# Gate and up weight units: transposed on VectorE instead of TensorE, in a quartered layout and a new schedule

## The reference

```
x = x + linear0(cond0(x))      cond0: rows of a sample times W[cond_id] (64 x 64)
                               linear0: x @ (W + sum of 8 LoRA products).T + bias, 1024 -> 1024
x = x + down(silu(gate(c)) * up(c)),   c = adapter(x): rank-16 product B, A of the sample's adapter id
gate, up: 2752 x 1024, down: 1024 x 2752, as NF4 codes (int32, 0 to 15):
    W[o, i] = NF4[codes[o, i]] * scales[o, i // 64]
```

## Time and profile before

| | |
|---|---|
| Median of three runs | 1036.76 us (1036.56 to 1037.09) |
| Profiled execution, its own time | 1037.4 us |
| Its span | 1035.5 us |
| First and last L948 start (phase A) | 41.1 and 349.4 us |
| Matmuls at L982 | 520 (65 units of 8) |
| VectorE L735, mean of one | 1233 ns, x260 |
| VectorE L737, mean of one | 1230 ns, x195 |
| ScalarE L566, mean of one | 1051 ns, x455 |
| DMA, mean over the span | 122 GB/s |

### The profile page before, as it was taken

How to read it: one execution, slowest core, us unless ns; L and a number is a source line. 1 busy time by engine, 2 the same in 40 slices (tenths; PEclk the granted TensorE clock), 3 DMA queues, 4 the chain that set the end, 5 groups by cost and what they waited for, 6 DMA issues and landing times.

```text
span 1035.5 us, 14607 instructions
## 1 busy us (share of the span) xinstructions
PE 1005.8 (97%) x5368; PEld 858.6 (83%) x5368; DVE 841.6 (81%) x834; ACT 793.5 (77%) x946; POOL 223.2 (22%) x269
## 2 busy tenths in 40 slices
PE   4999999999999899999999999999999999999998
PEld 3898898998898777788888888888888888888886
DVE  3999999989999889978887788887887879784344
ACT  4788887888888779888888888888887878884120
POOL 4014434324322301120111111111122112112000
PEclk9999999999999999999999999999999999999999
DMA  9844455446432436755654645655464545565666
GB/s 249 245 119 127 113 138 124 104 139 149 104 104 62 82 61 122 132 100 115 118 106 82 114 95 98 121 102 103 82 122 87 103 96 109 95 102 143 162 223 225
DMA packets 65397, 126.27 MB, mean 122 GB/s; under 512 B 6544, under 2 KB 38816, under 8 KB 65328
## 3 DMA queue, kind: packets, MB, share of 16 engines
q0 software_dynamic: 15200, 51.41, 31.9%
q1 hardware_dynamic: 48800, 72.88, 23.1%
q10 hardware_dynamic: 1328, 1.05, 0.3%
HBM read 66.61 MB, written 67.11 MB: 129 GB/s over the span
## 4 chain that ended last, share of the span: by engine, by line
PE 84%; DVE 9%; ACT 3%; issue 2%; DMA 1%; ACTq 0%; DVEq 0%
PE ps_z L1074 21%; PE ps_y L1074 21%; PE ps_z L948 13%; PE ps_gu L1053 11%; PE ps_t L982 5%; DVE val L735 4%; PE ps_t L990 3%; PE ps_gu L990 3%; DVE val L737 3%; PE ps_y L935 2%; PE ps_gu L965 2%; ACT ring L566 1%; PE ps_t L957 1%; DMA la<-in_L_ffn_lora_A 1%; DVE val L754 1%
## 5 line engine op out<-in xcount | busy, mean ns | idle before, releaser
L566 ACT ACTIVATE ring<-codes 128x1024 f32<-128x1024 int32 x455 | 452.6, 1051 | 17.9 <-DVE val L735 17.8
L735 DVE TENSOR_TENSOR val<-val,ring 128x1024 f32<-128x1024 f32 x260 | 320.6, 1233 | 36.3 <-ACT ring L566 20.4
L737 DVE SCALAR_TENSOR_TENSOR val<-ring,val 128x1024 f32<-128x1024 f32 x195 | 239.9, 1230 | 39.4 <-ACT ring L566 31.5
L539 POOL DMA_DIRECT2D out<-staged x80 | 68.8, 860 | 315.3 <-ACT staged L685 307.9
L866 DVE TENSOR_TENSOR inter<-ps_gu,inter 128x512 f32<-128x512 f32 x88 | 60.5, 687 | 74.5 <-ACT inter L671 74.5
L671 ACT ACTIVATE inter<-ps_gu 128x512 f32<-128x512 f32 x88 | 52.4, 595 | 71.8 <-PE ps_gu L1053 69.3
L948 PE MATMUL ps_z<-we_hi,y_hi 128*128 128x512 f32 x256 | 104.8, 409 | 0.5 <-DVE y_lo L785 0.5
L948 PE MATMUL ps_z<-we_hi,y_lo 128*128 128x512 f32 x256 | 100.4, 392 | 0.0
L948 PE MATMUL ps_z<-we_lo,y_hi 128*128 128x512 f32 x256 | 99.9, 390 | 0.0
L677 ACT ACTIVATE in_hi<-inter 128x512 fp32r<-128x512 f32 x88 | 55.4, 630 | 48.1 <-DVE inter L866 48.1
L481 POOL TENSOR_TENSOR st_hi<-ga_f,one 128x128 fp32r<-128x128 f32 x42 | 40.7, 968 | 218.1 <-ACT ga_f L606 218.1
(11 more groups left out here) (130 smaller groups left out, 1856.6 us busy)
## 6 DMA issues: line engine op xcount, KB each, us to landing
out<-staged POOLq DMA_DIRECT2D x80, 512.0 KB, 5.4
codes<-in_L_ffn_gate_codes SPq DMA_DIRECT2D x21, 512.0 KB, 4.9
codes<-in_L_ffn_up_codes SPq DMA_DIRECT2D x21, 512.0 KB, 4.2
codes<-in_L_ffn_down_codes SPq DMA_DIRECT2D x21, 512.0 KB, 4.0
xs<-in_x SPq DMA_DIRECT2D x16, 512.0 KB, 4.3
out<-in_L_ffn_bias SPq DMA_DIRECT2D x4, 2048.0 KB, 13.4
out<-xs POOLq DMA_DIRECT2D x16, 512.0 KB, 5.5
ring<-out SPq DMA_DIRECT2D x16, 512.0 KB, 4.6
```

The costliest lines, as they stand in the source:

```text
L539: pool.dma_start(out_rows[t * P:(t + 1) * P, :], staged[:, place, :], accum_op=ALU.add).then_inc(acc_out[place], 16)
L566: act.activation(ring[:, (k - 1) % RING, :], codes[:, n % 2, :], ACT.Identity, bias=offset, scale=slope).then_inc(lines, 1)
L735: ins = dve.tensor_tensor(v, v, line, pick)
L737: ins = dve.scalar_tensor_tensor(out=v, in0=line, scalar=add, in1=v, op0=ALU.add, op1=pick)
```

## The change

- A gate or up unit is loaded in quarters: partition block a (32 partitions) holds columns 256a to 256a + 255 of all 128 rows, rows i * 32 + p side by side. So each 32 x 32 block, transposed by VectorE's block transpose within its partitions, gives the columns on the partitions, in the layout that `adapter_ga` reads. The transpose is a ninth step of these units, for which `turn_unit` and `evac_wt` are gone. `wt` has two places, the ring four instead of five.
- The scales are needed in the same layout: they are loaded raw, and `place_scales` moves them by 32 small matmuls with slices of the identity in the setup; ScalarE copies them.
- Ten chunks in phase A instead of twelve: 22 units, 12 or 13 steps a tile, 9 in the setup. The other units are distributed over the groups.
- In phase B the steps of a slot come from a rate by group, `TURN_AT` follows from when a unit's steps are done. `gate_up`, `silu` and `product` move from the end of a slot, or the start of the next, into the middle of the slot; `inter_hi` and `inter_lo` stay in the next.
- TensorE's `adapter_ga` waits for `gu_turned` instead of `evicted`, and `cond_y` for `scales_ready`. The counts of `turned` and `evicted` count down units only.

The diff, cut to its core:

```diff
-    RING = COMBOS - 2
+    RING = COMBOS - 3
-    UNITS = [(kind, c) for c in range(12) for kind in "gu"]
+    UNITS = [(kind, c) for c in range(10) for kind in "gu"]
...
     BY_GROUP = [
+        [("d", 3), ("d", 4), ("g", 10), ("d", 5), ("u", 10), ("d", 6)],
+        [("d", 7), ("g", 11), ("d", 8), ("u", 11), ("g", 12), ("d", 9), ("u", 12), ("d", 10), ("g", 13)],
+        [("d", 11), ("u", 13), ("d", 12), ("g", 14), ("u", 14), ("d", 13), ("g", 15), ("d", 14), ("u", 15)],
+        [("d", 15), ("g", 16), ("u", 16), ("g", 17), ("u", 17), ("g", 18), ("d", 16), ("u", 18), ("d", 17), ("d", 18)],
...
+    STEP = [(n, op) for n, (kind, _) in enumerate(UNITS) for op in range(1, COMBOS + (2 if kind == "d" else 3))]
+    STEPS_SETUP = 9
+    STEPS_A = [12 + (t % 4 == 0) for t in range(NT)]
...
+    def lines_by(steps):
+        if steps >= len(STEP):
+            return NLINES * NU
+        n, op = STEP[steps]
+        return min(NLINES * n + min(op - 1, NLINES) + LEAD, NLINES * NU)
...
+    RATE = [3.9, 5.2, 5.2, 5.2, 5.4]
+    for slot in range(NT * (NG - 1)):
+        spare += RATE[slot // NT] - (slot - 1 in TURN_AT and UNITS[TURN_AT[slot - 1]][0] == "d")
+        steps = max(0, min(int(spare), len(STEP) - done))
...
+                    quarter = D // PQ
+                    for a in range(PQ):
+                        part = codes[a * SQ:(a + 1) * SQ, slot, :].rearrange("p (i j) -> p i j", i=PQ)
+                        cols = slice(a * quarter, (a + 1) * quarter)
...
+                            sp.dma_start(part, src[c * P:(c + 1) * P, cols].rearrange("(i p) j -> p i j", p=SQ)
+                                         ).then_inc(signal, 16)
...
@@ decode, VectorE
+                if op == COMBOS + 2:
+                    m = GU_NO[n]
+                    dve.wait_ge(scaled, n + 1)
+                    wait(dve, ga_mm, m - 1)
+                    quarters = v.rearrange("p (i j q) -> p q i j", i=PQ, q=DC)
+                    dve.transpose(wt[:, m % 2, :, :].rearrange("p q (i j) -> p q i j", i=PQ), quarters).then_inc(gu_turned, 1)
+                    return
...
@@ slot of phase B, ScalarE
+                    works = gate_ups_at(g, t // TPB, t % TPB)
                     if before is not None:
                         evac_unit(before)
-                    for work in works:
+                    for work in earlier:
                         inter_hi(*work)
                     if 0 < slot <= LAST:
                         evac_out(slot - 1)
                     some_lines(at, steps // 2)
+                    for work in works:
+                        silu(*work)
+                    some_lines(at + steps // 2, steps - steps // 2)
+                    if is_gu(before):
                         evac_ga(before)
...
@@ slot of phase B, VectorE
                     some_steps(at, min(steps, 1))
+                    for work in earlier:
                         inter_lo(*work)
                     if before is not None and UNITS[before][0] == "d":
                         low_wd(before)
...
+                    some_steps(at + 1, (steps + 1) // 2 - 1)
+                    for work in works:
+                        product(*work)
+                    some_steps(at + (steps + 1) // 2, steps // 2)
...
@@ TensorE
+            def place_scales():
+                pe.wait_ge(gu_scales_in, 16 * 4)
+                for kind, chunks in ((0, FULL + 1), (1, FULL)):
+                    to = ps_y[:, kind * HALF:kind * HALF + chunks * SB].rearrange("p (c i b) -> p i c b", i=PQ, b=SB // PQ)
+                    for a in range(PQ):
+                        for i in range(PQ):
+                            ins = pe.matmul(to[a * SQ:(a + 1) * SQ, i, :, :], ident[:, i * SQ:(i + 1) * SQ],
+                                            scales_raw[:, kind, 0:chunks, a * PQ:(a + 1) * PQ], start=i == 0, stop=i == PQ - 1)
+                ins.then_inc(scales_mm, 1)
...
-                    down(g, t, range(chunks - 1))
+                    down(g, t, range(chunks - 2))
+                    for work in gate_ups_at(g, t // TPB, t % TPB):
+                        gate_up(*work)
+                    down(g, t, range(chunks - 2, chunks - 1))
+                    if is_gu(before):
                         adapter_ga(before)
                     down(g, t, range(chunks - 1, chunks))
-                    for work in gate_ups_at(g, t // TPB, t % TPB):
-                        gate_up(*work)
                     if now is not None:
                         turn_unit(now, NT)
```

More of the change, by code:

```diff
@@ L108, in adaln_ffn @@
         PLACE_A[t, 0] = len(PLACE_A)
-        if 5 * t % 8 < 5:
+        if t % 8 in (0, 3, 6):
             PLACE_A[t, 1] = len(PLACE_A)
     assert len(PLACE_A) == PHASE_A_UNITS
[L112 to L115, removed]
+    for units in BY_GROUP:
         UNITS += units
@@ new lines, in adaln_ffn @@
+    TURN_AT, STEPS_B = {-1: PHASE_A_UNITS}, []
+    done, spare = STEPS_AT[NT], 0.0
+    for slot in range(NT * (NG - 1)):
+        spare += RATE[slot // NT] - (slot - 1 in TURN_AT and UNITS[TURN_AT[slot - 1]][0] == "d")
+        steps = max(0, min(int(spare), len(STEP) - done))
+        STEPS_B.append(steps)
+        spare, done = spare - steps, done + steps
+        n = max(TURN_AT.values()) + 1
+        if n < NU and DONE[n + 1] <= done - (0 if UNITS[n][0] != "d" else steps):
+            TURN_AT[slot] = n
@@ L569, in some_lines @@
             def some_lines(first, count):
-                for j in range(first, first + count):
+                for j in range(lines_by(first), lines_by(first + count)):
                     line(j // NLINES, j % NLINES)
[L574 to L579, removed]
             def evac_wd(n):
                 c = UNITS[n][1]
-                act.wait_ge(turned, n + 1)
+                act.wait_ge(turned, D_NO[n] + 1)
                 if c >= WD:
@@ L629, in _ @@
                            ps_t[:, :].rearrange("j (q p) -> j q p", q=DC), ACT.Copy).then_inc(setup_evac, 1)
-            some_lines(0, 2)
-            at = 2
+            for j in range(lines_by(0)):
+                line(0, j)
+            at = 0
             for jc in range(DC):
-                some_lines(at, 1)
-                at += 1
+                some_lines(at, STEPS_JC[jc])
+                at += STEPS_JC[jc]
                 if jc == DC - 1:
@@ L712, in _ @@
                     some_lines(at, steps // 2)
-                    if before is not None and UNITS[before][0] != "d":
+                    for work in works:
+                        silu(*work)
+                    some_lines(at + steps // 2, steps - steps // 2)
+                    if is_gu(before):
                         evac_ga(before)
-                    some_lines(at + steps // 2, steps - steps // 2)
                     at += steps
+                    earlier = works
         @block.vector
@@ L891, in _ @@
             inter_lo(0, 0, 2)
+            earlier = []
             for g in range(NG):
@@ L894, in _ @@
                     slot = NT * g + t
-                    works = gate_ups_at((slot - 1) // NT, (slot - 1) % NT // TPB, (slot - 1) % TPB) if slot else []
+                    works = gate_ups_at(g, t // TPB, t % TPB)
                     before = TURN_AT.get(slot - 1)
-                    steps = steps_by(slot) - steps_by(slot - 1)
-                    for work in works:
-                        product(*work)
+                    steps = STEPS_B[slot]
                     some_steps(at, min(steps, 1))
-                    for work in works:
+                    for work in earlier:
                         inter_lo(*work)
@@ L1006, in _ @@
                 add_lora(jc)
+                if jc == SCALES_JC - 1:
+                    place_scales()
                 if jc == 3:
```

122 lines of the change are left out of this document (63 added, 59 removed), and 4 rows, old and new, of the table BY_GROUP.

## The result

The changed kernel takes 1038.22 us (median of 20 runs) against 1037.06 before: ratio 1.0015, 95% interval 1.0008 to 1.0022. That is the same time to within 0.2%, where 1019 was forecast. One of the 20 runs was a slow one of 1994.93 us; the others lie between 1037.16 and 1039.75. The profiled execution has a span of 1036.6 us.

A forecast was written before the change was run, and what follows sets the result against it. TensorE was taken to bound the kernel, phase A having VectorE full too. Stages 41.1 + 5.5 + 291 + 110 + 495 + 75.3 = 1017.9 us of span, so 1019; range 998 to 1046.

The forecast's parts named there:

- The transpose's 1.25 us: VectorE's 128x1024 transpose with a 32-byte read step: 1.25 us each, 1.20 from start to start, bounds 0.69 and 2.02.
- The first rival: On VectorE, a transpose costs 2.0 us like L812; 38 in phase A and groups 0 to 3 add 30 us: 1049; chance 0.2.
- the two cases: TensorE stays the bound, 993 us, chance 0.12; or 0.83 us stalls follow VectorE into groups 1 to 3, 1046, chance 0.13.
- TensorE's side: 43 gate and up turns of 0.87 us leave TensorE, 37 us, the whole possible gain; setup's scale matmuls add work.
- Phase A: VectorE becomes longer than TensorE (281 us): 291 us, a gain of 17.5, with 22 units instead of 26.
- Groups 1 to 4: VectorE, at 1.27 us a step, binds groups 1 to 3 by 2 us each; total 495, as before.
- My claim that turns saved would be paid back in decoding: In groups 1 to 4, 17 turns saved are paid back in four extra units' decoding and the transposes; 495 us unchanged.
- Change-over and group 0: VectorE's 0.83 us stalls for ring lines should go with the mid-slot order: 110 us for the 115.6.
- Tail: Group 5 and tail: a ring of four places still covers the loads, so nothing changes, 75.3 us.
- Setup: 64 exposed scale-matmul passes on TensorE add 5.5 us (4.9 to 7.1); VectorE's ninth step lies in idle time.
- my lower bound of 0.077: Setup: a scale-matmul pass of 88 columns takes at least 88 / 128 of 0.11 us, 0.077.
- Third rival: VectorE's 0.83 us stall follows into groups 1 to 3, in 12 slots of 16: 27 us more, 1046; chance 0.13.
- Transfers: Gate or up loads as four of 128 KB on SP fit; landing in 5 us or less, x loads wait 1 us longer.

The follow-up runs named there:

- flat read: Changed kernel with one line altered: the transpose reads 32 neighbouring elements instead of every eighth, so the output is not the reference's; 999.74 us, ratio 0.9643.
- the order alone: Kernel before, with gate_up, silu and product moved to mid-slot and in_hi, in_lo in the next; units, turns and rates unchanged; 1029.59 us, ratio 0.9933.
- the late loads: Changed kernel with correct contiguous transpose reads, the adapters' A loads issued after the last W load and awaited only by the first ga product; 997.57 us.
- the old order: Phase B slot order of before, put into the changed kernel (stepped reads, 1094.57 us) and into the one with correct contiguous reads (1057.85 us).
- relaid: Changed kernel with contiguous transpose reads made right: columns dealt out otherwise, adapters' A loaded in that order by 32 small loads; 1001.63 us, ratio 0.9662.

## Why the prediction was wrong

The time that was forecast is 19 us off. One term is to blame, the price of the transpose: 38 of them on the engine that binds, each 0.89 us longer from start to start than forecast, are 34 us, and the flat read, which changes nothing but their read, gave back 38.5 (1038.22 to 999.74). Other terms, off the other way by some 15 us together, hid part of it. By stage, changes in us from before:

```
                       forecast    after    flat read
setup                      +5.5     +3.4         +3.1
phase A                   -17.5     -1.7        -18.0
change-over, group 0       -5.6     -9.9        -14.1
groups 1 to 4                 0    +11.0         -7.8
group 5 and tail              0     -1.8         -1.9
sum                       -17.6     +1.0        -38.7
```

- **The transpose's 1.25 us: the step that failed.** It is 2.16 (2.09 from start to start). The contiguous transpose is what I took, 1.24. My two reasons for calling the stepped read cheap were both unsound: L628 shows that a stepped write alone takes 2.0 on ScalarE, not that a stepped read doesn't; and TensorE's weight loads (188 against 141 ns) are another engine's reads, and the bound of 1.50 us that I took from them was exceeded. The first rival had the mechanism (2.0 us, by L812), at a chance of 0.2. Its time, 1049, was 11 too high, for the other terms below. The range 998 to 1046 held the measured time by luck: it came from neither of the two cases that it was meant to cover.
- **TensorE's side: right.** Its busy time fell by 26.4 us, where 37 for turns less 3 for the scales is 34. With the flat read, which gives TensorE the same work, it fell by 34.6 (971.2 us on its page). So no term of work was missing; the 8 us came with the slow transposes (busy time also holds matmuls at the lower clock and modelled ends), and I didn't take them apart. Its sums for groups 1 to 3 were met to 0.3 us by the flat read.
- **Phase A: right as a sum.** 291 with the contiguous transpose, measured 290.3. VectorE is the longer engine there in all versions with the transposes: TensorE stands for y_lo 21.5 us after the change and 6.6 with the flat read.
- **Groups 1 to 4: a VectorE step was mis-sized.** I took 1.27 us from phase A. After, groups 1 to 3 are 379.9 us of a full VectorE; less 16 transposes x 2.09, 96 x 0.60, 11 x 1.13 leaves 276.5 for 223 steps, 1.24. In the kernel with the flat read that brings VectorE just under TensorE (365.1 against 365.7), and groups 1 to 4 take 485.0 us, TensorE's own sum (484.8). My claim that turns saved would be paid back in decoding was so only with the slow transpose.
- **Change-over and group 0: right in kind, too small.** The forecast was 5.6. Up to TensorE's first down pass of group 1 it is 115.6 us before, 112.1 with the order alone and 105.2 after: the order gave 3.5, the rest of the change 6.9 more, in spite of two slow transposes.
- **Tail: 75.3 forecast, 73.5 measured.** The order alone does it (73.4), by what means I didn't look into.
- **Setup: a right time from two wrong terms.** It is 3.4 us longer, where 5.5 for the scales were forecast. The 64 passes took 3.0 us (L1012, 24.66 to 27.72), 0.047 each, below my lower bound of 0.077. That bound scaled a pass with 128 stationary columns by its moving columns, and these passes have 32 stationary ones. Of the 3.0 only 1.4 reach the end of the setup (VectorE's we_lo at 39.40 instead of 38.01), mostly since in this profile the chunk of W before them was begun 1.8 us earlier (22.26 against 24.02). The other 2.0 are the first unit's transpose. I had put VectorE's ninth step into its idle time, but it stands in the chain, in front of the y_lo for which phase A waits. With the fast transpose and the late loads the setup is 43.7, 0.8 us shorter. The matmuls in order of time, then three pieces of the chain of waits (start us, us, what):

```profile
24.66 3.06 PE L1012 MATMUL ps_y<-scales_raw,ident 128*32 128x88 f32 x64
...
40.62 1.14 DVE val L787
41.79 2.05 DVE wt L770
43.84 1.17 DVE y_lo L818 x2
```

- **Third rival (the 0.83 us follow VectorE): the mechanism is real, and the change had removed it.** I gave it 27 us in groups 1 to 3; with the old order these groups take 34 more (413.8 against 379.9), and the whole kernel 56. So with this distribution of steps the 43 units on VectorE pay only together with the new order: with the old order they make the kernel slower than before even with fast transposes (1.0213, 1.0196 to 1.0230).
- **Transfers:** four loads of 128 KB landed in 3.9 and 2.9 us instead of 4.9 and 4.2. ScalarE stood 2.0 us for them in all, in two places, where it had no such wait before.

## What to carry to other kernels

When an operation that no row shows decides the bound, a row with two differences (a stepped read and a stepped write) prices both until something separates them; another engine's row does not. If the layout is free, choose which element goes to which partition so that the inner loop is contiguous: here it was worth 3.5% (1038.22 to 1001.63 us), and 3.9% once its small loads were out of the way. And moving work to a nearly full engine asks first for an order in which the engines don't wait for each other in turn inside a slot.

## What the runs showed of the hardware

- In float32 VectorE slows down between a step of 8 and one of 16 bytes: a transpose takes 1.25 us contiguous and with step 2, 1.99 with step 4 and 2.01 with step 8 in the read. A copy takes 0.69, 0.69 and 1.07 us (contiguous, steps 2 and 4). ScalarE, tried at 16 and 32 bytes, takes 2.04 against 1.06.
- In the kernel the same stepped transpose takes 2.16, alone 2.01; the contiguous one 1.24 in both. Why, no run shows.
- TensorE's granted clock stood at 1.2 GHz in some stretches; those looked at here came after a wait. In the profile after, TensorE waited 1.43, 1.40 and 0.35 us at the change-over, and then matmuls of 0.39 us took 0.63. The stretches below show it (columns as in the earlier trace rows; 0.50 is the clock), first after, then relaid, behind the wait of 2.57 us in the setup. But a wait is not enough by itself: the kernel before waited 1.9 us for the same ga_f at the change-over as the kernel with the mid-slot order did (which then stood at 0.50 from 354.8 to 361.6 us), and kept 1.00. No run tried this by itself.

```profile
358.00:361.00 3.00, 3.00 (x11) 2.51 (x11) 0.23 (x1) 1.03 (x3) 0.00 (x0) 0.50 0.95 156
...
38.40:41.80 3.40, 3.40 (x14) 2.92 (x13) 1.10 (x1) 0.00 (x0) 1.06 (x2) 0.50 1.02 365
```
